# Moving the output part's loads of contexts and x from SyncE's queue to ScalarE's

## The reference

```
xn = layernorm(x)
s = attention(xn) @ W_o                      # softmax(q k^T / 4) v per head, with rotary positions
g = silu(ffn(xn))                            # expert = argmax(router(xn)); h = leaky(x W_fc)^2; h W_proj
out = x + s * g
```

## Time and profile before

| | us |
|---|---|
| median of 3 runs | 2382.63 (2381.94 to 2383.34) |
| the profiled execution | 2382.36 |
| its span, first to last instruction | 2380.6 |
| output part (first gather to the end of the span) | 205 |

### The profile page before, as it was taken

The page is one execution under the profiler, slowest core; times in us unless marked ns, Lnnn a source line. Parts: engine busy times, 40 slices in busy tenths (PEclk is TensorE's granted clock), DMA queues, the critical chain, the costliest instruction groups (busy, mean ns, idle before and its releaser), DMA issues. The chain is left out here.

```text
span 2380.6 us, 86989 instructions
## 1 busy us (share of the span) xinstructions
PE 2243.9 (94%) x34337; PEld 1250.7 (53%) x34349; DVE 2041.1 (86%) x5699; ACT 1729.4 (73%) x4127; POOL 972.1 (41%) x1126
## 2 busy tenths in 40 slices
PE   7999994999999999999999999999999998998877
PEld 6777771444444444444444444444444445786655
DVE  7999989899999999999999999999999993744646
ACT  6777771888888888888888888888888886552000
POOL 6999996112223233232322323223232223224645
PEclk9999995999999999999999999999999999999999
DMA  6989885555543534434353443434444324896998
GB/s 216 293 291 301 299 277 165 167 185 199 174 126 108 153 104 133 126 118 143 105 177 115 128 133 110 147 105 135 125 125 135 108 80 125 299 323 206 285 281 292
DMA packets 258007, 423.53 MB, mean 178 GB/s; under 512 B 33728, under 2 KB 168128, under 8 KB 257472
## 3 DMA queue, kind: packets, MB, share of 16 engines
q1 hardware_dynamic: 245312, 384.41, 50.9%
q0 software_dynamic: 12288, 33.57, 4.2%
HBM read 226.50 MB, written 189.79 MB: 175 GB/s over the span
## 5 line engine op out<-in xcount | busy, mean ns | idle before, releaser
L934 DVE CUSTOM_DVE_ANT_0 dump<-ps_rows,mask 128x384 bf16<-128x384 f32 (+7 forms) x2048 | 1462.7, 755 | 108.9 <-issue 95.7
L909 ACT ACTIVATE probs<-ps_cols 128x512 f32<-128x512 f32 (+3 forms) x3072 | 1313.4, 498 | 214.7 <-PE ps_cols L1047 202.9
L1047 PE MATMUL ps_cols<-q_st,k_st 99*32 99x512 bf16 (+3 forms) x12288 | 881.0, 328 | 5.9 <-DMA q_st<-max_T 3.1
L994 PE MATMUL ps_rows<-k_st,q_st 96*32 96x384 bf16 (+3 forms) x12288 | 823.5, 331 | 15.4 <-DVE row_max L934 7.6
L881 POOL TENSOR_SCALAR_AFFINE_SELECT probs<-probs 128x512 f32<-128x512 f32 x512 | 325.5, 636 | 1105.2 <-ACT probs L909 1105.2
L1023 PE MATMUL ps_ctx<-probs,v_st 128*32 128x512 f32 (+3 forms) x6144 | 630.9, 486 | 0.9 <-POOL probs L881 0.8
L1047 PEld LDWEIGHTS ps_cols<-q_st,k_st 99*32 99x32 bf16 x12288 | 316.6, 95 | 402.2 <-ACT probs L909 258.6
L994 PEld LDWEIGHTS ps_rows<-k_st,q_st 96*32 96x32 bf16 x12288 | 280.7, 95 | 377.0 <-DVE row_max L934 281.0
L1023 PEld LDWEIGHTS ps_ctx<-probs,v_st 128*32 128x32 f32 x6144 | 166.0, 110 | 58.0 <-POOL probs L881 2.4
L934 DVE DVE_READ_ACCUMULATOR2_ANT row_max<- 128x1 f32 x2048 | 171.2, 84 | 0.1
L1363 PE MATMUL ps_t<-w_o_sb,cT 128*128 128x256 f32 x512 | 126.3, 403 | 33.4 <-DVE cT L1282 33.4
(11 more groups left out here) (115 smaller groups left out, 2195.5 us busy)
## 6 DMA issues: line engine op xcount, KB each, us to landing
parts_dram<-parts SPq DMA_DIRECT2D x64, 768.0 KB, 4.1
q_st<-parts_dram SPq DMA_DIRECT2D x384, 128.0 KB
k_st<-parts_dram SPq DMA_DIRECT2D x384, 128.0 KB
ctx_dram<-ctx_raw SPq DMA_DIRECT2D x128, 256.0 KB, 3.8
xs_dram<-zeros SPq DMA_DIRECT2D x36, 512.0 KB, 4.9
xs_sb<-xs_dram SPq DMA_DIRECT2D x72, 256.0 KB, 6.7
g_dram<-g_sb SPq DMA_DIRECT2D x72, 256.0 KB, 5.9
v_dram<-v_sb SPq DMA_DIRECT2D x32, 544.0 KB, 5.0
```

The costliest lines, as they stand in the source:

```text
L909: nc.scalar.activation(probs[:, k % PB, h, 0:w], ps_cols[(GH * k + h) % CB][:, 0:w], ACT.Exp).then_inc(exp_done, 1)
L934: nc.vector.tensor_tensor_reduce(out=dump[:, done % 2, 0:n], in0=ps_rows[:, 512 * bank:512 * bank + n], in1=mask[:, S - n:S], scale=1.0, s ...
L994: mm = nc.tensor.matmul(ps_rows[a:a + VW, 512 * (bank + c):512 * (bank + c) + w], q_st[r][0:KS, i // IB, q0 + a:q0 + a + VW], k_st[r][0:KS ...
L1047: mm = nc.tensor.matmul(ps_cols[(GH * k + h) % CB][a:a + VW, 0:w], k_st[r][:, j // IB, k0 + a:k0 + a + VW], q_st[r][:, c, h * 512 + q0 - 5 ...
```

## The change

SyncE's loop of the output part keeps only the stores and the wait for each result. The two loads go to ScalarE, behind its last gated block, in the order and with the waits they had. The loads that SyncE makes during the expert part stay on SyncE; the helper functions only take the issuing engine as an argument.

```diff
+    def load_ctx(eng, t):
+        rows = ctx_dram[t].rearrange("g (h e) t -> (g h) e t", h=GH)
+        for c in range(DC):
+            eng.dma_start(c_sb[:, t % CR, c], rows[c * H // DC:(c + 1) * H // DC, 0:HD]).then_inc(c_loaded[t % CR], 16)
+
+    def load_x(eng, t):
+        eng.dma_start(r_sb[:, t % XR].rearrange("p (s d) -> p s d", s=SUB),
+                     x[t].rearrange("(s p) d -> p s d", p=P)).then_inc(x_loaded[t % XR], 16)
...
         for t in range(NT):
-            n = t + CR
-            if n < NT:
-                sp.wait_ge(cT_ready, DC * (t + 1))
-                load_ctx(n)
             sp.wait_ge(out_ready, 2 * (t + 1))
             sp.dma_start(out[t].rearrange("(s p) d -> p s d", p=P),
                          r_sb[:, t % XR].rearrange("p (s d) -> p s d", s=SUB)).then_inc(out_stored[t % XR], 16)
-            n = t + AHEAD
-            if XR <= n < NT:
-                sp.wait_ge(out_stored[n % XR], 16 * (n // XR))
-                load_x(n)
...
     @block.scalar
...
+        for t in range(NT):
+            n = t + CR
+            if n < NT:
+                act.wait_ge(cT_ready, DC * (t + 1))
+                load_ctx(act, n)
+            n = t + AHEAD
+            if XR <= n < NT:
+                act.wait_ge(out_stored[n % XR], 16 * (n // XR))
+                load_x(act, n)
```

More of the change, by code:

```diff
@@ L1139, in load_xs @@
                 .then_inc(xs_loaded[n % XS], 16)
[L1141 to L1144, removed]
         def load_sums():
@@ L1149, in load_sums @@
             sp.dma_start(sums, rows[:, :, HD]).then_inc(sums_loaded, 16)
-        def load_x(t):
-            sp.dma_start(r_sb[:, t % XR].rearrange("p (s d) -> p s d", s=SUB),
-                         x[t].rearrange("(s p) d -> p s d", p=P)).then_inc(x_loaded[t % XR], 16)
         for n in range(NBLK):
@@ L1162, in _ @@
             if n % 4 == 3 and n // 4 < CR:
-                load_ctx(n // 4)
+                load_ctx(sp, n // 4)
             if n == SUMS_AT:
@@ L1168, in _ @@
             if n >= NBLK // 2 and n % 4 == 1 and (n - NBLK // 2) // 4 < XR:
-                load_x((n - NBLK // 2) // 4)
+                load_x(sp, (n - NBLK // 2) // 4)
         for t in range(NT):
-            n = t + CR
-            if n < NT:
-                sp.wait_ge(cT_ready, DC * (t + 1))
-                load_ctx(n)
             sp.wait_ge(out_ready, 2 * (t + 1))
```

## The result

The change makes the kernel faster: 2370.40 us (2367.54 to 2371.95, 5 runs) against 2381.94 (2381.03 to 2383.34, 5 runs), a ratio of 0.9949, 95% interval 0.9934 to 0.9963. That is 11.5 us; I had forecast 2 and called it no change. Run again beside other kernels it gave 0.9963 (0.9950 to 0.9975).

A forecast was written before the change was run, and what follows sets the result against it. The prediction took the eight DMA engines carrying context loads as the bound, if always the same eight. Its terms, -4.1 + 4.6 - 2.5 = -2.0 us, gave 2380.6 us, called no change, range 2370 to 2388.

The forecast's parts named there:

- step 4: Output part: earlier issue is worth nothing where the eight engines are full, but gains 4.1 us in the emptier start.
- first rival: Middle stage: a second queue raises the eight engines' rate, 6.75 us a tile, 2371 us; chance 0.25.
- Steps 1 to 3: Load queue: issuing on ScalarE costs and gains 0; contexts and x come a tile earlier, leads 3.08 and 1.54 us.
- Step 5: End of slow stage: stores with their own queue get three further ahead by x(21), making it 4.6 us later.
- Step 6: Tail from tile 24, paced by GpSimd's issuing: fewer stores left and x further ahead, gain 2.5 us.

The follow-up runs named there:

- stores_on_act: Against the kernel before: stores moved to ScalarE's queue, all loads left on SyncE's without the wait for a result; 0.9949.
- one_queue_spread: Against the kernel before: one queue, second half of each context load issued behind the store instead of ahead of it; gained nothing.
- ctx_alone_x_first: Against the kernel before: contexts on ScalarE; x and stores on SyncE, x of tile t + 4 issued ahead of store t; gained 0.5%.
- by_parity: Against the kernel before: even tiles' transfers all on SyncE, odd tiles' all on ScalarE; gained 0.5%.
- one_queue_x_first_again: Against the kernel before: one queue, x of tile t + 4 issued ahead of store t instead of behind it, a repeat run; 0.9970.
- ctx_alone: Against the kernel before: only context loads moved to ScalarE, x loads left on SyncE behind the stores; nothing gained in the time.
- one_queue_ctx_between: Against the kernel before: one queue, order store, contexts, x instead of contexts, store, x, no load earlier; 0.9980.

## Why the prediction was wrong

- **What bounds the kernel: right in the main.** Eight engines carry each context load, and giving it 16 took 7.69 us a tile to 5.79. That the uneven spread was the bound is shown; that they are the same eight each time fits it, but no view names the engines.
- **The step that failed is 4, through the price that it rests on.** "In a stage where the eight engines are full it is worth nothing: the same bytes have to go through." I had priced those bytes at 21.3 GB/s an engine, the rate at which they went, and took it for what a full engine can do. It was the rate under one order of transfers. After the change the eight carry 0.164 MB in 6.72 us, 24.4 GB/s, which is the 24.3 that the earlier trace rows had shown at its best. The stage of tiles 10 to 21 gave 10.7 us where I had put 0. The 4.1 us that step 4 did count, for loads moved into the emptier start, came out as 0.7 at tile 10: it had no term for the first gathers, whose wait grew by 3.0 us.
- **The first rival named the stage, the size and the time** (6.75 us a tile, 2371), at a chance of 0.25, but not the reason. It took the gap for idling. Filling idle time at the old packet cost would have shown as a share of 1.06; it was 0.95, with shorter packets. A part may be filling all the same, by the shares of 0.90 with one queue and 0.95 with two at one packet cost.
- **The argument against it misled me.** SyncE's held-up issues show that some queue was full, and so that engines were busy. They don't show that busy engines could not be quicker. The Trainium skill ("DMA: Bandwidth & Descriptors", "Issuing engines are not separate DMA queues") says that several issuing engines save only the time of issuing. The runs differ from that, and they decide: the second queue took the window from 280 to 320 GB/s. What the queues hold, and in what order, moved the time by 0.2 to 0.5%, while it did not matter which of the two engines had the loads (stores_on_act, 0.9949).
- **Steps 1 to 3: right.** ScalarE issued four context loads from 2172.05 and x of tile 6 at 2188.78 (forecast about 2176 and 2190, in a profile shifted by 2.2 us), and 2174 to 2184 moved 195 GB/s, not 139 (177 in 2172 to 2182, the window shifted along). Held behind the old results it still gained 0.35% (0.9965), so the lead is worth little; its share can't be told from the intervals.
- **Step 5: not seen as a cost.** I had put the end of the slow stage 4.6 us later; tile 21's add came at 2312.39, not at about 2326. Stores landed in 8.5 us at the median, not in 4 to 6. What their own queue cost the loads can't be read beside the faster stage.
- **Step 6: too large.** The tail gave 0.8 us, not 2.5. GpSimd's last 32 gathers took 40.7 us, before 41.2.

What is shown: the gain does not come from the lead, and a part of it comes from order alone, in one queue (0.9980). On 8 engines, with the order contexts-x-store, or with x and stores in different queues, a kilobyte costs 47 to 48.1 ns in every kernel measured; with x loads behind stores in one queue it costs 50 to 53. On 16 engines it is 52.7 with x directly behind the store and 48.6 with them apart. one_queue_spread, with half a context load between store and x, stays at 50.9.

What stays open: why a packet is longer when an x load follows a store in its queue; how ctx_alone_x_first gains 0.5% with long packets, and by_parity with packets in between (both are marked *); and how much of the change's gain is the second queue as such. The last is the first rival in a weaker form. That freeing x from the results helps by itself, beyond the order, fits one_queue_x_first_again (0.9970 against 0.9980), but the intervals overlap.

## What to carry to other kernels

A high busy share of the DMA engines does not say that they are at their best: divide the share by the bytes and compare it with the best stretch of the same trace (53 ns a kilobyte against 1.08 x 16 / 388 = 44.5 here). If it is higher, try another order of loads and stores in the queue, and a second queue. Judge them by the time: on 16 engines shorter packets gained nothing. Read the time of a part from its first to its last operation, since a stage that looks faster can have its slow stretch moved ahead of it (ctx_alone). Count the small packets per transfer: where they show fewer than 16, reordering a transfer's dimensions so that it spreads over all engines was worth more than any shuffling of queues (1.1% against 0.5%). And when a held-up queue is the evidence that a move can't help, ask what sets the rate at which it drains.

## What the runs showed of the hardware that I had not expected

The same transfers cost 53 ns of packet time per kilobyte or 47, by their order in one queue (the kernel before 53.1, one_queue_ctx_between 47.2), with the same sizes and the same waits in another order. A context load whose outer dimension is 8 heads ended on 8 engines, and with 16 positions outermost on 16 (3616 small packets in the window against 3376, with four gated blocks fewer in it). The issue of a context pair grows from 1.2 or 1.3 us to 4 us and more when its queue is backed up, on SyncE (5.16) and on ScalarE alike (4.46, 6.68), and that of an x load from 0.4 or 0.5 us to 1.85 and 1.49. It holds up only what that engine issues: in the change SyncE's stores went out in 0.37 to 0.39 us each beside ScalarE's 4.46. Four context loads of 8 engines issued at once lengthen the wait for gathers issued beside them: the first gate was waited for 9.65 us and not 6.66.
